# Router logits from the first normalised tile, and a regrouped TensorE sequence

## The chip, the core and the metric

One core of a Trainium2 chip runs the whole program in one launch. The metric is device time in microseconds, the median of three runs.

## The reference

For 128 batches of 128 tokens with 256 features the reference computes a pre-normalised cross attention with a residual, and then a routed feed-forward block with a residual:

```
x = x + attention(layernorm(x), ctx) @ Wo.T + bo      # 16 heads of 16, softmax
h = layernorm(x)
e = argmax(h @ router_w.T + router_b)                  # one of 32 experts per token
x = x + relu(relu(h @ w1[e] + b1[e]) @ w2[e] + b2[e])
```

## The kernel before

The program has an attention stage and a page stage. The attention stage goes over 32 quads `q` of four batches. Its step `s` attends quad `s`, one batch `u` at a time, and in the same step prepares quad `s+1` (keys, queries, values), normalises `s+2`, and routes earlier quads. Each engine's order is written out by hand in a loop over `s` and `u`, with semaphores between engines (`after` waits until a semaphore has counted up to a quad and an index).

In one batch TensorE (loop at L876) does, in this order: scores for the maxima, second half (`scores_for_max(s, u, 1)`, L791, bf16); the exact scores (L806); the first half of probabilities times values of the batch before (`attend`, L824, into bank `pB`); `max_transpose` (L798), which turns the maxima so that they can be subtracted; the second half of `attend`; `subtract_max` (L815); the first half of the next batch's scores for maxima; three of six matmuls of one projection (`project`, L774); transposes of a normalised tile (L765, into bank `sc0`) in some batches; the values of one batch (L782); and in one batch of four the transpose of the logits (L844) or the ranks (L849 to L853). Then come the output projection (`project_out`, L832) and the other three matmuls of the projection.

VectorE (loop at L689) does per batch: `maxima` of the second half (L595, two reductions), `attended` and `normalise` (transpose L615, reciprocal L619, product `nrm` L621 of two SBUF tiles, transpose L626 to `aT`), `maxima` of the next batch's first half, the low half of the transposed tile (`xnT_lo`, L610: bank minus high half), and `residual` (L604), which adds the projected attention to `xs` and stores `row`. Behind the residual stand, by batch, `stats1` (L586, L589), `slot_sum`, `best` with `choose` (L633 to L645), or `scan` (L649).

ScalarE does the exponentials (L468), the copies out of PSUM (L457, L472, L479, L482), both normalisations (`norm1` L435, `norm2` L444) and the squares for the second one (L452). GpSimd (loop at L393) does `rstd1` and `rstd2` (inverse deviations, L281 to L302), `split` (L316, L318: high and low parts of the context), `add_bo` (L308: output bias added to `xs`), the slot arithmetic (`fresh_pages`, `place`), and `scatter` (L386), which writes the rows to pages of one expert each in DRAM. SyncE issues the loads and fills pages.

The second layer norm is applied in full (`norm2`), its tile is transposed (`xn2T`), and `logits` (L838) multiplies it by the router's weights. Logits of quad `q` are taken in step `q+2`; its rows are scattered in step `q+3`. When all rows are placed, the page table is read (L249) and the page stage runs 160 pages through their experts.

The order of TensorE around the change:

```
project(pq, n, (0, 1) if s < 0 else (0,))      # L942
...
values(s + 1, u)                               # L965
...
project_out(q1, u1)                            # L982
project(pq, n, (1,))                           # L984
```

Of the kernel before, what the change touches and what calls it, by code (L numbers as in the profile page):

```python
# [18 lines left out]
QB = 4  # L19
ROW = 260  # L20
COL_TOKEN, COL_EXPERT, COL_MEAN, COL_RSTD = 256, 257, 258, 259
# [32 lines left out]
def build(nc, x, ctxT, wq, wk, wv, wo, bq, bk, bv, bo, wr, rb, w1, w2, consts, out):  # L54
# [14 lines left out]
    with ctx:  # L69
# [6 lines left out]
        def sem(name):  # L76
# [4 lines left out]
        wo_s = sb("wo_s", [2, D])  # L81
# [3 lines left out]
        bv_s, bo_s, rb_s = sb("bv_s", [D]), sb("bo_s", [D]), sb("rb_s", [E])  # L85
        bvT = sb("bvT", [2, P])
        rb4, rbp = sb("rb4", [QB, E]), sb("rbp", [1])
# [3 lines left out]
        xs = sb("xs", [4, QB, D])  # L91
        row = sb("row", [4, QB, ROW])
        xn, xn2 = sb("xn", [QB, D]), sb("xn2", [QB, D])
        xnT = sb("xnT", [2, 2, QB * P], F32R)
        xn2T = sb("xn2T", [2, QB * P])
# [14 lines left out]
        sq2 = sb("sq2", [2])  # L110
# [33 lines left out]
          bvT_done bvT_out bo_done bo_out rbT_done rbp_out rb4_out  # L144
          S_done T_done PV_done O_done V_done proj_done mxT_done xnT_done xn2T_done lg_done lgT_done rk_done
          exp_out V_out proj_out xnT_out xn2T_out lgs_out rk_out xn_out xn2_out
          max_out mxT_out tr_out inv_out nrm_out aT_out x2_out sq_out stat1_out agg1_out xnTl_out
          lg_out top_out eq_out pick_out idx_out hot_out scan_out slot_out
          var1_out pow1_out mr1_out rstd1_out mean2_out sq2_out eps2_out var2_out pow2_out rstd2_out
# [14 lines left out]
        def live(q):  # L164
            return 0 <= q < NQ
# [11 lines left out]
        def xn2T_bank(h):  # L177
            return sc[2 * h]

# [8 lines left out]
        def _(sp):  # L188
            def load_x(q, u):
                sp.dma_start(xs[:, q % 4, u], x[q * QB + u]).then_inc(S[f"ld_x{q % 4}_{u}"], 16)  # L190
# [14 lines left out]
            for dst, src in ((bq_s[:, :], bq), (bk_s[:, :], bk), (bv_s[:, :], bv), (bo_s[:, :], bo), (rb_s[:, :], rb)):  # L205
                sp.dma_start(dst, src).then_inc(S["ld_b"], 16)
            sp.dma_start(wo_s[:, :, :], wo).then_inc(S["ld_wo"], 16)
            for u in range(QB):
                load_x(1, u)
            sp.dma_start(wr_s[:, :, :], wr).then_inc(S["ld_wr"], 16)  # L210
# [11 lines left out]
            load_ctx(3, 0)  # L222
            load_ctx(3, 1)

            for q in range(NQ):
                for u in range(QB):
                    after(sp, "x2_out", 4, q, u)
                    if u == 3 and q >= 2:
                        after(sp, "scattered", 64, q - 2, 63)
# [837 lines left out]
```

## Time and profile before

| | |
|---|---|
| median of three runs (lowest, highest) | 1223.89 us (1223.77, 1226.08) |
| the profiled execution: its time, its span | 1223.15 us, 1221.3 us |
| busy share TensorE, VectorE, ScalarE, GpSimd | 90%, 76%, 70%, 69% |
| chain that ended last | PE 60%, DVE 20%, POOL 7%, DMA 5%, issue 4%, ACT 3% |
| attention stage, its drain, page stage | to about 964, to about 999, to 1221 us |
| granted TensorE clock, mean of the span | 0.972 of full speed |

The chain of waits is followed back from the last instruction; its shares say which engine's work the end hangs on. In the timeline an instruction has its start from the span's beginning and its duration; instructions overlap by their pipelines, so what one costs its engine is the distance to the next start. Matmuls in fp32 take two records each in some groups. A wait stands in brackets, with what ended it.

### The profile page before, as it was taken

The numbers are of one execution on the slowest core, as the hardware profiler recorded it, in microseconds if no ns is written. First come the engines' busy times: TensorE is split into PE (matmuls) and PEld (weight loads), VectorE is DVE, ScalarE is ACT, GpSimd is POOL, SyncE is SP. The second block draws the span as 40 slices with busy tenths as digits, with TensorE's granted clock in tenths as the row PEclk, the third lists the DMA queues.
The fourth block names the chain that finished last, engine by engine and source line by source line (L and its number), as shares of the span: only waits on it lengthen the run. The fifth ranks groups of instructions, "written<-read, shape, count | busy, mean of one in ns | idle before, by whom it ended". The sixth has DMA issues, their size and how long they took to land.

```text
span 1221.3 us, 39225 instructions
## 1 busy us (share of the span) xinstructions
PE 1097.5 (90%) x15399; PEld 845.1 (69%) x15399; DVE 925.0 (76%) x2321; ACT 858.5 (70%) x2020; POOL 847.3 (69%) x1613
## 2 busy tenths in 40 slices
PE   5999999999999999999999999999998419998893
PEld 4777777777777777777777777777776319977772
DVE  4787888888888888888888888888877427866772
ACT  4777777777777777777777777777776306655551
POOL 4544777677777777777777777777764656777776
PEclk9999999999999999999999999999999859999997
DMA  7415222522222222222222222222110136676650
GB/s 243 147 56 121 71 72 71 142 80 76 76 73 79 82 83 75 80 71 72 72 78 74 72 71 72 71 72 72 59 41 29 52 132 205 198 215 205 205 161 17
DMA packets 91156, 120.40 MB, mean 99 GB/s; under 512 B 14096, under 2 KB 73883, under 8 KB 90781
## 3 DMA queue, kind: packets, MB, share of 16 engines
q1 hardware_dynamic: 77150, 84.04, 24.2%
q0 software_dynamic: 13824, 33.85, 7.7%
q8 instruction: 124, 2.03, 0.7%
q14 instruction: 58, 0.48, 0.1%
HBM read 60.61 MB, written 59.31 MB: 98 GB/s over the span
## 4 chain that ended last, share of the span: by engine, by line
PE 60%; DVE 20%; POOL 7%; DMA 5%; issue 4%; ACT 3%; SPq 1%; POOLq 0%; DVEq 0%; ACTq 0%
PE pB L832 10%; PE pA L774 9%; PE pB L824 8%; PE sc L782 7%; DVE mx L595 6%; PE sc L806 5%; POOL out L419 4%; PE sc L765 4%; PE sc L815 3%; ACT arena L468 3%; DVE nrm L621 3%; PE m L791 3%; PE sc L1000 3%; DMA out<-arena 2%; PE m L798 2%
## 5 line engine op out<-in xcount | busy, mean ns | idle before, releaser
L595 DVE TENSOR_REDUCE mx<-m 128x4 bf16<-128x512 f32 x512 | 322.6, 670 | 10.7 <-PE m L791 10.5
L468 ACT ACTIVATE arena<-sc 128x512 f32<-128x512 f32 x512 | 264.5, 603 | 47.5 <-PE sc L815 47.5
L419 POOL DMA_INDIRECT out<-arena x160 | 157.0, 981 | 60.9 <-issue 31.1
L615 DVE STREAM_TRANSPOSE tr<-pB 128x512 f32<-128x512 f32 x128 | 91.8, 717 | 106.3 <-PE pB L824 106.3
L806 PE MATMUL sc<-qk 32*128 32x256 f32 x2048 | 167.0, 397 | 0.5 <-DVE rbp L674 0.5
L824 PE MATMUL pB<-arena 128*32 128x128 f32 x4096 | 159.8, 276 | 1.5 <-issue 1.0
L386 POOL DMA_INDIRECT pages<-row,slot_i x128 | 130.4, 1019 | 40.0 <-issue 37.0
L832 PE MATMUL pB<-wo_s,aT 128*128 128x256 f32 x512 | 138.0, 392 | 8.7 <-DVE aT L626 8.7
L824 PEld LDWEIGHTS pB<-arena 128*32 128x32 f32 x4096 | 99.0, 109 | 44.6 <-issue 43.6
L774 PE MATMUL pA<-cHi,wqkv 128*128 128x512 f32 x252 | 119.0, 474 | 9.4 <-DVE wqkv L660 9.4
L774 PE MATMUL pA<-xnT,wqkv 128*128 128x512 f32 x372 | 124.7, 443 | 0.0
L554 ACT ACTIVATE arena<-sc 128x256 f32<-128x256 f32 x160 | 61.5, 384 | 84.8 <-PE sc L991 81.8
L504 ACT ACTIVATE mxT<-m 128x128 bf16<-128x128 f32 x128 | 35.6, 278 | 115.9 <-PE m L798 115.9
L806 PEld LDWEIGHTS sc<-qk 32*128 32x128 f32 x2048 | 115.4, 186 | 0.7 <-ACT arena L472 0.7
L782 PE MATMUL sc<-wqkv,cHi 128*128 128x256 f32 x512 | 108.3, 303 | 2.5 <-ACT arena L468 0.9
L832 PEld LDWEIGHTS pB<-wo_s,aT 128*128 128x128 f32 x512 | 89.2, 194 | 21.3 <-DVE aT L626 14.6
L791 PE MATMUL m<-qk 32*128 32x128 bf16 x2048 | 101.8, 216 | 1.9 <-ACT qk L482 1.8
L1000 PE MATMUL sc<-arena,xs 128*128 128x128 f32 x640 | 99.1, 278 | 0.0
L791 PEld LDWEIGHTS m<-qk 32*128 32x128 bf16 x2048 | 63.5, 93 | 48.8 <-issue 46.3
L352 POOL TENSOR_TENSOR step_d<-run,ends 128x32 f32<-128x32 f32 x32 | 8.1, 254 | 128.1 <-DVE run L649 128.1
L734 DVE TENSOR_SCALAR arena<-arena 128x256 f32<-128x256 f32 x160 | 71.0, 444 | 32.0 <-DMA arena<-pages 31.7
L991 PE MATMUL sc<-cst,arena 128*128 128x128 f32 x320 | 62.8, 279 | 30.5 <-DVE arena L734 30.2
(141 smaller groups left out, 2714.9 us busy)
## 6 DMA issues: line engine op xcount, KB each, us to landing
arena<-pages SPq DMA_DIRECT2D x160, 130.0 KB
cT<-ctxT SPq DMA_DIRECT2D x64, 256.0 KB, 3.8
xs<-x_in SPq DMA_DIRECT2D x128, 128.0 KB, 3.3
pages<-empty SPq DMA_DIRECT2D x120, 130.0 KB, 3.1
pages<-empty SPq DMA_DIRECT2D x1, 5200.0 KB, 19.8
out<-arena POOLq DMA_INDIRECT x160
w2s<-w SPq DMA_DIRECT2D x1, 2080.0 KB
qk<-w SPq DMA_DIRECT2D x1, 2064.0 KB, 8.2
```

The costliest lines, as they stand in the source:

```text
L386: pool.indirect_dma_start(pages, bass.IndirectOffsetOnAxis(slot_i[:, u:u + 1], 0), row[:, q % 4, u, :], None, bounds_check=last_slot, oob_ ...
L419: pool.indirect_dma_start(out_rows, bass.IndirectOffsetOnAxis(pr[:, r, COL_TOKEN:COL_TOKEN + 1].bitcast(U32), 0), pr[:, r, 0:D], None, bou ...
L468: act.activation(pt[:, u % 2, g].rearrange("p i k -> p (i k)"), sc[g][:, :], ACT.Exp).then_inc(S["exp_out"], 1)
L595: ins = dve.tensor_reduce(mx[:, 32 * g:32 * g + 4], mb[i][:, :].rearrange("p (h k) -> p h k", h=4), AX.X, ALU.max)
L615: dve.transpose(tr[:, :], pB[:, :]).then_inc(S["tr_out"], 1)
L774: ins = pe.matmul(proj_bank(q, n)[:, :], wqkv[:, w, a, i, c * P:(c + 1) * P], src[:, i, :], start=(i == 0 and (a, b) == HI_LO[0]), stop=(i ...
L782: ins = pe.matmul(sc[1][:, 0:D], (cHi, cLo)[a][:, q % 2, i, u * P:(u + 1) * P], wqkv[:, 2, b, i, :], start=(i == 0 and (a, b) == HI_LO[0]) ...
L791: ins = pe.matmul(mb[i][:, j * P:(j + 1) * P], qMh[rows, q % 2, m, c, u * P:(u + 1) * P], kTh[rows, q % 2, c, u * P:(u + 1) * P], start=Tr ...
L806: pe.matmul(dst, kT[rows, q % 2, c, u * P:(u + 1) * P], qM[rows, q % 2, :, c, u * P:(u + 1) * P], start=(c == 0), stop=False, skip_group_c ...
L824: ins = pe.matmul(pB[32 * g:32 * g + 32, j * P:(j + 1) * P], vs[:, q % 2, u, h, :], pt[:, u % 2, g, j, :], start=True, stop=True)
L832: ins = pe.matmul(pB[:, 0:D], aT[:, i, :], wo_s[:, i, :], start=(i == 0), stop=(i == 1))
L1000: ins = pe.matmul(sc[2 + n % 2][:, 0:P], w1p[:, n % W1R, i * HID:i * HID + P], pnT[:, n % DEEP, i * P:(i + 1) * P], start=(i == 0), stop=( ...
```

## The change

The router's logits are no longer computed from the second normalised tile. With the router's weights centred over the features, the mean of the second layer norm drops out of the product, and its inverse deviation can be multiplied in afterwards:

- Setup: `centre_router` subtracts from `wr_s` its mean over features and then over experts. `wo_s` gets 32 more columns, the product of the output weights and the centred router weights; `bo_s` gets 32 more, the bias times the router weights. These products, with their transposes and copies, stand in step -1 on TensorE and VectorE.
- Quad `q`'s first normalised tile, transposed in fp32 (`xnTf`), is multiplied by the router's weights in step `q-1`, batch 1, transposed, multiplied by the deviation (`sd1`, new in `rstd1`), and stored beside `x` in `xs` (`x_logits`, VectorE).
- `project_out` has 288 columns instead of 256, and `residual` adds 288: the last 32 are logits without the scale. `best` multiplies them by `rstd` and adds the router's bias: two more VectorE instructions. `add_bo` adds 288 columns.
- `norm2`, its eight transposes per quad, `xn2T_copy` and `logits_across` go. `squares` writes to a tile of its own.
- `xnT_copy` is two instructions: bank to `xnTf`, `xnTf` to `xnT`; `xnT_lo` subtracts from `xnTf` in SBUF, no longer from the bank.
- All six matmuls of a projection stand together ahead of the values, and the output projection is last in a batch.
- Routing comes one quad earlier: logits' use, ranks and `place` in step `q+1`, scatter in step `q+2`. `rstd2` works on four batches at once. `slot_sum`, `choose`, `scan` and the statistics of batches 0 and 1 move to the place behind the second maxima.
- Rows have their four columns of metadata in front of `x`, not behind it.

```
 def rstd1(q):
     ...
+    pool.tensor_tensor(sd1[:, q % 2, :], v, r, ALU.mult).then_inc(S["std1_out"], 1)
...
 for s in range(-1, NQ + 2):                                    # GpSimd, after
+    if live(s - 2):
+        slots_as_integers(s - 2)
+        scatter(s - 2)
+    if live(s - 1):
+        rstd2(s - 1)
     if s >= 0 and live(s + 2):
         split(s + 2)
     if live(s + 1):
         add_bo(s + 1)
+    if live(s - 1):
+        meta(s - 1)
+    if live(s + 3):
+        rstd1(s + 3)
+    if live(s - 1):
+        fresh_pages(s - 1)
+        place(s - 1)
...
 def xnT_copy(q, h):                                            # ScalarE
-    act.activation(xnT[:, 0, :, 2 * P * h:2 * P * (h + 1)], xnT_bank(q, h)[:, :].rearrange("p (c t) -> p c t", c=2),
-                   ACT.Copy).then_inc(S["xnT_out"], 1)
+    act.activation(xnTf[:, :, at], xnT_bank(q, h)[:, :].rearrange("p (c t) -> p c t", c=2), ACT.Copy).then_inc(S["xnTf_out"], 1)
+    after(act, "xnTf_out", 2, q, h)
+    act.activation(xnT[:, 0, :, at], xnTf[:, :, at], ACT.Copy).then_inc(S["xnT_out"], 1)
...
+def x_logits(q):                                               # VectorE
+    after(dve, "lgT_done", 1, q, 0)
+    after(dve, "std1_out", 1, q, 0)
+    if q >= 4:
+        after(dve, "x2_out", 4, q - 4, 3)
+    dve.tensor_tensor(xs[:, q % 4, :, D:D + E], sc[3][:, 0:P].rearrange("p (u e) -> p u e", e=E),
+                      sd1[:, q % 2, :].unsqueeze(2).to_broadcast([P, QB, E]), ALU.mult).then_inc(S["lg_out"], 1)
...
 def best(q):
-    after(dve, "lg_out", 1, q, 0)
+    after(dve, "rstd2_out", 1, q, 0)
+    if q >= 1:
+        after(dve, "eq_out", 1, q - 1, 0)
+    own("scaled_out", q + 1, dve.tensor_tensor(lg[:, :, :], row[:, q % 4, :, X0 + D:X0 + D + E],
+                                               row[:, q % 4, :, COL_RSTD].unsqueeze(2).to_broadcast([P, QB, E]), ALU.mult))
+    own("z_out", q + 1, dve.tensor_tensor(lg[:, :, :], lg[:, :, :], rb_s[:, :].unsqueeze(1).to_broadcast([P, QB, E]), ALU.add))
...
         maxima(s, u, 1)                                        # VectorE's loop
+        if u == 0 and live(s - 2):
+            slot_sum(s - 2)
+        if u == 2 and live(s - 1):
+            choose(s - 1)
+        if u == 3 and live(s - 1):
+            scan(s - 1)
+        if u < 2 and live(s + 3):
+            stats1(s + 3, (u,))
...
 def project_out(q, u):                                         # TensorE
-        ins = pe.matmul(pB[:, 0:D], aT[:, i, :], wo_s[:, i, :], start=(i == 0), stop=(i == 1))
+        ins = pe.matmul(pB[:, 0:D + E], aT[:, i, :], wo_s[:, i, :], start=(i == 0), stop=(i == 1))
...
-        project(pq, n, (0, 1) if s < 0 else (0,))
+        project(pq, n)
...
-    if live(pq) and s >= 0:
-        project(pq, n, (1,))
```

VectorE between batch 1's residual and batch 2's attention, before (names are tiles; `m` and `pB` are PSUM banks, `row` the stored rows, `lg` logits, `mx` maxima):

```order
L604 SCALAR_TENSOR_TENSOR row<-pB,xs 128x256 [waits scattered,xb_out,O_done]
L633 TENSOR_REDUCE top<-lg 128x4 [waits lg_out]
L634 TENSOR_TENSOR eq<-lg,top 128x128 [waits top_out]
L639 TENSOR_TENSOR eq<-eq,cst 128x128 [waits eq_out]
L642 TENSOR_REDUCE idx<-eq 128x4 [waits expert_out,pick_out]
L645 TENSOR_TENSOR hot<-cst,idx 128x128 [waits own_slots,idx_out]
L595 TENSOR_REDUCE mx<-m 128x4 [waits S_done]
L595 TENSOR_REDUCE mx<-m 128x4
L615 STREAM_TRANSPOSE tr<-pB 128x512 [waits PV_done]
```

and now:

```order
L570 SCALAR_TENSOR_TENSOR row<-pB,xs 128x288 [waits scattered,xb_out,O_done]
L609 TENSOR_TENSOR lg<-row 128x128 [waits eq_out,rstd2_out]
L611 TENSOR_TENSOR lg<-lg,rb_s 128x128 [waits scaled_out]
L612 TENSOR_REDUCE top<-lg 128x4 [waits z_out]
L613 TENSOR_TENSOR eq<-lg,top 128x128 [waits top_out]
L561 TENSOR_REDUCE mx<-m 128x4 [waits S_done]
L561 TENSOR_REDUCE mx<-m 128x4
L618 TENSOR_TENSOR eq<-eq,cst 128x128 [waits eq_out]
L621 TENSOR_REDUCE idx<-eq 128x4 [waits expert_out,pick_out]
L624 TENSOR_TENSOR hot<-cst,idx 128x128 [waits own_slots,idx_out]
L581 STREAM_TRANSPOSE tr<-pB 128x512 [waits PV_done]
```

Four instructions, two of them new, stand between residual and maxima, and the last three of the choice stand behind the maxima.

VectorE between batch 2's residual and batch 3's attention, now (before, `scan` stood at the end of batch 3, behind its residual and the statistics of one batch):

```order
L570 SCALAR_TENSOR_TENSOR row<-pB,xs 128x288 [waits O_done]
L552 BN_STATS st<-xs 128x6 [waits ld_x3_2,agg1_out]
L552 BN_STATS st<-xs 128x6 [waits ld_x3_3]
L555 BN_AGGR ag<-st 128x2 [waits stat1_out] x2
L561 TENSOR_REDUCE mx<-m 128x4 [waits S_done]
L561 TENSOR_REDUCE mx<-m 128x4
L628 SCALAR_TENSOR_TENSOR run<-fresh,run,zer 128x32 [waits fresh_out]
L581 STREAM_TRANSPOSE tr<-pB 128x512 [waits PV_done]
```

The `scan` now stands ahead of the attention's transpose and waits for GpSimd's `fresh`.

GpSimd from the end of `place` to the scatter, before:

```order
L281 TENSOR_SCALAR rs<-ag 128x4 [waits xn_out,agg1_out]
L283 TENSOR_TENSOR rs<-rs,half 128x4 [waits var1_out]
L285 TENSOR_TENSOR nm<-ag,rs 128x4 [waits pow1_out]
L287 TENSOR_SCALAR nm<-nm 128x4 [waits mr1_out]
L316 CAST cHi<-cT 128x1024 [waits V_done,ld_c1,ld_c0]
L318 TENSOR_TENSOR cLo<-cT,cHi 128x1024 [waits ctx_hi]
L376 CAST slot_i<-slot 128x4 [waits slot_out,scattered]
L308 TENSOR_TENSOR xs<-xs,bo_s 128x1024 [waits xn_out]
```

and now, from the end of `rstd2` to `rstd1`, with `fresh_pages` next:

```order
L296 TENSOR_TENSOR row<-row 128x4 [waits pow2_out]
L311 CAST cHi<-cT 128x1024 [waits V_done,ld_c1,ld_c0]
L313 TENSOR_TENSOR cLo<-cT,cHi 128x1024 [waits ctx_hi]
L303 TENSOR_TENSOR xs<-xs,bo_s 128x1152 [waits lg_out,xn_out]
L320 TENSOR_SCALAR expert<-idx 128x4 [waits idx_out]
L322 CAST row<-tok 128x4 [waits tok_out]
L324 CAST row<-expert 128x4 [waits expert_out]
L325 TENSOR_SCALAR tok<-tok 128x4
L274 TENSOR_SCALAR vr<-ag 128x4 [waits lg_out,xn_out,agg1_out]
L276 TENSOR_TENSOR rs<-vr,half 128x4 [waits var1_out]
```

`split` and `add_bo` follow directly on `rstd2`, and `rstd1` stands between them and `fresh_pages`.

## Rows read from the trace of the kernel before

**Rows 1.** Timeline, GpSimd and VectorE: start us, us, engine line op out<-in, count.

```profile
531.80 2.39 POOL L308 TENSOR_TENSOR xs<-xs,bo_s 128x1024 f32<-128x1024 f32 x1
...
533.26 1.21 DVE L621 TENSOR_TENSOR nrm<-tr,inv 128x256 f32<-128x256 f32 x1
...
855.53 1.22 DVE L621 TENSOR_TENSOR nrm<-tr,inv 128x256 f32<-128x256 f32 x1
```

**Rows 2.** Timeline of TensorE over two batches, [idle before it <-releaser].

```profile
524.23 0.24 PE L798 MATMUL m<-ident_b,mx 128*32 128x128 bf16 x4
...
526.64 0.60 PE L765 MATMUL sc<-cst,xn 128*128 128x128 f32 x4
...
527.82 0.33 PE L844 MATMUL sc<-cst,lgs 128*128 128x128 f32 x1
...
527.98 1.03 PE L832 MATMUL pB<-wo_s,aT 128*128 128x256 f32 x4
...
531.47 0.24 PE L798 MATMUL m<-ident_b,mx 128*32 128x128 bf16 x4
...
532.65 0.96 PE L774 MATMUL pA<-xnT,wqkv 128*128 128x512 f32 x3
...
533.45 0.60 PE L765 MATMUL sc<-cst,xn 128*128 128x128 f32 x4
...
533.80 0.48 PE L782 MATMUL sc<-wqkv,cHi 128*128 128x256 f32 x2
...
539.36 0.24 PE L798 MATMUL m<-ident_b,mx 128*32 128x128 bf16 x4 [0.69 <-DVE mx L595]
```

**Rows 3.** Timeline of VectorE in the same quad.

```profile
528.29 0.69 DVE L610 TENSOR_TENSOR xnT<-sc,xnT 128x512 fp32r<-128x512 f32 x1 [0.19 <-ACT xnT L457]
...
529.05 0.42 DVE L604 SCALAR_TENSOR_TENSOR row<-pB,xs 128x256 f32<-128x256 f32 x1
...
536.53 0.28 DVE L633 TENSOR_REDUCE top<-lg 128x4 f32<-128x128 f32 x1
...
538.02 1.28 DVE L595 TENSOR_REDUCE mx<-m 128x4 bf16<-128x512 f32 x2
...
540.11 0.72 DVE L615 STREAM_TRANSPOSE tr<-pB 128x512 f32<-128x512 f32 x1 [0.81 <-PE pB L824]
...
541.98 1.25 DVE L595 TENSOR_REDUCE mx<-m 128x4 bf16<-128x512 f32 x2
...
543.95 0.42 DVE L604 SCALAR_TENSOR_TENSOR row<-pB,xs 128x256 f32<-128x256 f32 x1 [0.72 <-PE pB L832]
...
545.18 1.26 DVE L595 TENSOR_REDUCE mx<-m 128x4 bf16<-128x512 f32 x2
```

**Rows 4.** Timeline of TensorE at the start: six projection matmuls in one stretch.

```profile
18.71 1.56 PE L774 MATMUL m<-xnT,wqkv 128*128 128x512 f32 x6
```

**Rows 5.** Timeline of GpSimd, and one row of ScalarE, in the same quad.

```profile
526.09 0.45 POOL L281 TENSOR_SCALAR rs<-ag 128x4 f32<-128x4 f32 x1
...
528.22 1.04 POOL L316 CAST cHi<-cT 128x1024 fp32r<-128x1024 f32 x1
...
529.84 0.22 ACT L452 ACTIVATION_READ_ACCUMULATOR xn<-row 128x1 f32 x1
...
543.38 0.25 POOL L337 TENSOR_TENSOR need<-rks,room 128x32 f32<-128x32 f32 x1 [1.00 <-ACT rks L500]
...
544.15 0.30 POOL L341 TENSOR_SCALAR fresh<-fresh 128x32 f32<-128x32 f32 x1
```

**Rows 6.** Timeline of TensorE, and a 2 us stretch of the drain (busy time, PEclk, DMA).

```profile
936.41 0.33 PE L844 MATMUL sc<-cst,lgs 128*128 128x128 f32 x1 [1.93 <-ACT arena L468]
...
938.00:940.00 2.00, 2.00 (x25) 1.33 (x23) 1.47 (x5) 0.54 (x3) 0.73 (x2) 0.50 0.00 0
```

**Rows 7.** Timeline of the drain: last output projection, read of the page table.

```profile
963.63 1.13 PE L832 MATMUL pB<-wo_s,aT 128*128 128x256 f32 x4 [0.81 <-DVE aT L626]
...
999.46 0.58 SPq L249 DMA_DIRECT2D arena<-pages  x1
```

More of the change, by code:

```diff
@@ L392, in _ @@
             split(1)
-            for s in range(-1, NQ + 3):
-                if live(s - 1):
-                    rstd2(s - 1, 0)
-                if live(s - 3):
-                    place(s - 3)
-                if live(s + 2):
-                    rstd1(s + 2)
+            rstd1(1)
+            for s in range(-1, NQ + 2):
+                if live(s - 2):
+                    slots_as_integers(s - 2)
+                    scatter(s - 2)
+                if live(s - 1):
+                    rstd2(s - 1)
                 if s >= 0 and live(s + 2):
                     split(s + 2)
-                if live(s - 3):
-                    slots_as_integers(s - 3)
                 if live(s + 1):
                     add_bo(s + 1)
-                if live(s - 3):
-                    if live(s - 1):
-                        after(pool, "sq_out", 4, s - 1, 3)
-                    scatter(s - 3)
                 if live(s - 1):
-                    rstd2(s - 1, 1)
-                if live(s - 2):
-                    meta(s - 2)
-                    fresh_pages(s - 2)
+                    meta(s - 1)
[4 more added lines that the diff above has]
+                    place(s - 1)
             for n in range(PAGES):
@@ L538, in _ @@
                             norm1(s + 2, v)
-                    if u in (0, 2) and live(s - 1):
-                        norm2(s - 1, u)
-                        norm2(s - 1, u + 1)
                     if live(q1):
@@ L688, in _ @@
             query_masks()
-            for s in range(-2, NQ + 3):
+            for s in range(-2, NQ + 2):
                 for u in range(QB):
@@ new lines, in output_bias, with router_weights @@
+                ins.then_inc(S["setup_products"], 1)
+                for c in range(2):
+                    for i in range(2):
+                        ins = pe.transpose(sc[2][:, (2 * c + i) * P:(2 * c + i + 1) * P], wo_s[:, i, c * P:(c + 1) * P], ident)
+                ins.then_inc(S["setup_products"], 1)
+            def router_weights():
+                pe.wait_ge(S["wr_centred"], 4)
+                pe.wait_ge(S["setup_copies"], 2)
+                for c in range(2):
+                    for i in range(2):
+                        ins = pe.matmul(sc[0][:, c * E:(c + 1) * E], won_s[:, i, c * P:(c + 1) * P], wr_s[:, i, :],
+                                        start=(i == 0), stop=(i == 1))
+                ins.then_inc(S["setup_products"], 1)
+                pe.wait_ge(S["bo_out"], 1)
+                for c in range(2):
+                    ins = pe.transpose(pB[:, c * P:(c + 1) * P], bo_s[:, c * P:(c + 1) * P], ident)
+                ins.then_inc(S["setup_products"], 1)
+                logits(0)
+                after(pe, "lgs_out", 1, 0, 0)
+                logits_transpose(0)
@@ L872, in _, with router_bias @@
+            def router_bias():
+                pe.wait_ge(S["setup_copies"], 4)
+                for i in range(2):
+                    ins = pe.matmul(pB[:, D:D + E], boT[:, i, :], wr_s[:, i, :], start=(i == 0), stop=(i == 1))
+                ins.then_inc(S["setup_products"], 1)
             pe.wait_ge(S["ld_cst"], 16)
@@ L930, in _ @@
                     if live(pq):
-                        if u == 0 and live(s - 2):
-                            after(pe, "lgs_out", 1, s - 2, 0)
+                        if u == 1 and s >= 0 and live(s + 1):
+                            after(pe, "lgs_out", 1, s + 1, 0)
                         elif s >= 0:
```

306 lines of the change are left out of this document (136 added, 170 removed).

## The prediction

> **What bounds the kernel now.** Read the busy shares and the chain of waits first: TensorE is the busiest engine and carries most of the chain, so only what lengthens or shortens its sequence, or makes it wait, counts. The stage repeats every four batches (a quad): the same VectorE instruction stands at 533.26 and, 11 quads on, at 855.53 [rows 1], so a quad takes 29.30 us. Then read one quad instruction by instruction. My mark is M(u), the moment when TensorE transposes the maxima of batch u (L798), since everything later in the batch hangs on it: M(0) at 524.23, M(1) at 531.47, M(2) at 539.36 [rows 2]. M(2) stands behind a wait of 0.69 for VectorE, which ran five small routing instructions in front of the maxima (536.53 to 538.02) [rows 3]. So VectorE is the second bound, met once in a quad. GpSimd has time to spare, but holds VectorE once in a quad, 26 times in all: `nrm`, 0.42 us long elsewhere, takes 1.21, and ends 0.28 after GpSimd's `xs` addition (531.80 + 2.39 = 534.19, against 534.47) [rows 1]. The runs' median is 1223.89; the profiled execution took 1223.15, and sums are made against that.
>
> **TensorE's own work.** From M to the row transposes are 1.98 us with three projection matmuls (531.47 to 533.45) and 2.41 with logits (524.23 to 526.64), so logits cost 0.43; four transposes 0.35 (533.45 to 533.80); the transpose of logits 0.16 (527.82 to 527.98); and of the 3.75 from M(0) to the output projection, 0.83 are left for the values [rows 2]. Six projection matmuls in one stretch take some 1.50 (1.56, the last one's tail partly hidden [rows 4]), against 0.80 for three (532.65 to 533.45): 0.70 more before the output projection, and not after it. The change takes out eight of the transposes in a quad (0.70) and adds 32 columns to the output projection: an eighth of about 0.68, 0.08 a batch. It puts logits into batch 1. From M to the output projection I get 1.98 + 0.70 + 0.83 = 3.51, and so: u0 and u3, with transposes, 3.86; u1, with logits and their transpose, 4.10; u2, with the ranks (an estimate of 0.20, by the 0.16 of the one transpose), 3.71.
>
> **VectorE behind it.** Before, the second half of a projection stood behind the output projection and covered the residual. That cover is gone. The residual starts 1.07 after the output projection's start (527.98 to 529.05), 1.15 with the wider one, and lasts 0.42; the second maxima and their transpose follow in 1.34 (538.02 to M at 539.36) [rows 2, 3]. This is 2.91 from an output projection to the next M, in every batch. Between residual and maxima stand, after u1, the four instructions of `best` (of five in 1.49, so 1.2), and after u2 two statistics (543.95 to 545.18 less the residual: 0.81) [rows 3]. `choose`, `slot_sum`, `scan` and the other statistics move into the idle 0.75 after the maxima (539.36 to 540.11) [rows 2, 3] and cost nothing while that holds. From M to M:
> u0 3.86 + 2.91 = 6.77; u1 4.10 + 2.91 + 1.20 = 8.21; u2 3.71 + 2.91 + 0.81 = 7.43; u3 6.77. Sum 29.18 against 29.30: taken alone, the change is worth 0.1 a quad. The removed work on ScalarE (norm2 and its copies) gains nothing, as ScalarE already waits for TensorE. Its longer path now (squares behind the residual, then the projection's copy) ends near or before the next M, so I cost it at nothing, at most 0.3 a quad.
>
> **The scan waits for GpSimd (u3).** `scan` stands between maxima and the attention's transpose and needs `fresh`, which GpSimd makes behind `rstd1`, and that needs the statistics that end when the maxima of u3 start, 1.3 before M(3). `rstd1` takes 2.13 (526.09 to 528.22) and its new product 0.2; `fresh` 1.07 (543.38 to 544.15 and 0.30) [rows 5]. So `fresh` is there 2.1 after M(3), scan takes 0.25, and the transpose starts at 2.35 rather than 0.75. It and the first maxima take 3.12 (540.11 to 541.98, and 1.25), the remainder of `xnT` 0.69, residual 0.42, maxima 1.34 [rows 3]: M(0) of the next quad comes 7.92 after M(3). **+1.15 a quad.**
>
> **`best` meets the addition of the bias (u1).** Counted from M(0): the residual of the last batch starts at 3.86 + 1.15 = 5.0, its squares are summed 1.0 later (529.05 to 529.84 + 0.22) [rows 3, 5], and then `rstd2` runs for four batches at once: six small instructions with one power, by the four of `rstd1` about 2.6, to 8.6. `split` takes 3.45 (528.22 to 531.80, less a cast), to 12.0; the addition to `xs` 2.39 x 1152/1024 = 2.69, to 14.7 [rows 1, 5]. VectorE: M(1) 6.77, output projection 10.87, residual 12.0, so `best` begins at 12.45 with a product of two SBUF tiles, as `nrm` is. The addition is 0.4 under way. If the product waits as `nrm` did, it ends at 14.98 and not 12.74: **+2.24 a quad**. The three behind it and the maxima wait in turn, and TensorE with them. The Trainium skill says this as a rule (SBUF — State Buffer, "Who interferes with whom"): VectorE with two SBUF inputs and GpSimd reading SBUF lock each other out for a whole instruction. By that rule the remainder of `xnT`, which now reads SBUF twice, would also wait for one of `place`'s short instructions in u3, 0.2 to 0.4 a quad more; the trace shows only the long GpSimd instructions doing it.
>
> **The clock.** From the output projection to the next M TensorE itself needs 3.49 less the second half of the projection (527.98 to 531.47, less 0.70) [rows 2], so 2.8; M(2) now comes 2.91 + 1.20 + 2.24 = 6.35 after it. TensorE is idle for 3.5 us before M(2). Nothing like it stands in the main stage, where the granted clock is 1.00. In the drain an idle 1.93 us (before 936.41) is followed by a stretch at 0.50 (938 to 940) [rows 6], that is 1.2 GHz. Those 2 us cost 1.0 where TensorE sets the pace, and it does between M(2) and M(3). Bounds are 0 and 2.0; I take **+1.4 a quad**. The Trainium skill (TensorE: Matmul & The Clock Gate, "Why this matters for your kernels") warns of idle gaps between bursts of matmuls, after which the clock falls back. By that rule every quad has such a fall, as in my sum; the trace agrees in one place, outside the main stage.
>
> **Start and drain.** The start gains setup products, transposes and copies in a ring between TensorE, VectorE and ScalarE: 0 to 8, taken as 4 (twelve small matmuls at the price of the transposes, 1.1, and a few hand-overs). In the drain 35.8 us pass from the last output projection to the read of the page table (963.63 to 999.46) [rows 7]. Routing now runs one quad earlier and without norm2, eight transposes and late logits: statistics 2, rest of a scatter 1.5, `rstd2` 2.6, `best` and `choose` 2.1, ranks 1.2, `fresh_pages` and `place` 5.2, last scatter and landing 8: some 22.5. **-13**, bounds -6 and -18. The page stage is untouched. SyncE's context loads move in its queue and now wait for `split` of the same step (12.0); the next `split` starts some 30 later, so they stay covered.
>
> **Sum.** Quads 1 to 28 have both waits: 28 x (-0.12 + 1.15 + 2.24 + 1.40) = 28 x 4.67 = 131. Quad 29 has the addition but not `rstd1`: about 3. 1223.15 + 131 + 3 + 4 - 13 = **1348 us**.
>
> **Rivals.**
> - Faster, the other side: neither wait bites. `best` passes freely if the addition is over by 12.45 or begins after 13.7, so if GpSimd is 2.3 earlier or 1.7 later than I count; and the scan costs nothing if VectorE's slack takes it. Then 1223.15 - 28 x 0.12 + 4 - 13 = 1211; were VectorE never late, TensorE alone (3.9 + 2.8 a batch, near 26.8 a quad, in 28 quads) would give 1144. For: GpSimd idles enough, and my count has ten steps. Against: both gaps are larger than any step's error, and the lock came in nearly every quad. 0.20.
> - Only the scan waits: 1223.15 + 28 x 1.03 - 9 = 1243. For: `best`'s operands differ in shape from `nrm`'s. 0.13.
> - Both waits, clock stays at 1.00: 1223.15 + 28 x 3.27 + 2 - 9 = 1308. For: the one case at hand is from the drain, where TensorE had little else to do. 0.20.
> - Both, and the low clock lasts through u3 too (2.5 to 3 a quad): 1385. 0.07.
> - The gains and losses cancel within 0.2% of 1223.9 (what a measurement of this kernel can tell from no change): 0.02.
>
> **How the numbers follow.** The forecast gets 0.38, and by itself lies between 1325 and 1375. Slower is 0.38 + 0.13 + 0.20 + 0.07 = 0.78, faster 0.20, same 0.02. The range leaves out the faster half of the faster cases and most beyond 1385: 1205 to 1385.
>
> **What would show it.** Right: a period near 34 us; the first product of `best` lasting 2.3 to 2.6 and ending just after GpSimd's addition; scan idle some 2 us behind `fresh`; each maxima transpose in u2 behind a wait above 3 us; the granted clock under 1.00 in the main stage; the page table read about 22 after the last output projection. Wrong: a period under 29.3, `best` at 0.3 an instruction, or TensorE without waits at M.

## The result, and the profile of the changed kernel

| | before | changed |
|---|---|---|
| median, timed side by side (lowest, highest) | 1224.93 us (1223.77, 1226.08) | 1362.42 us (1357.60, 1362.93) |
| ratio, with its 95% interval | | 1.111 (1.109 to 1.114) |
| the profiled execution: time, span | 1223.15, 1221.3 us | 1362.93, 1361.1 us |
| M(0) to M(0), quads 2 to 27, mean | 29.35 us | 34.05 us |
| granted TensorE clock, mean of the span | 0.972 | 0.936 |

The change makes the kernel 11% slower; 1348 was forecast, 1205 to 1385 the range. The page of the changed kernel has TensorE's busy share down by 7 points, and VectorE with nearly a third of the chain of waits (20% before). These are its busy shares, its row of granted clock in 40 slices, and its chain by engine and by line:

```profile
PE 1125.3 (83%) x15164; PEld 861.5 (63%) x15164; DVE 1028.3 (76%) x2424; ACT 808.2 (59%) x1860; POOL 823.5 (61%) x1453
...
PEclk9999999999999998999999999999999876999997
...
PE 42%; DVE 30%; POOL 10%; issue 8%; DMA 6%; ACT 4%; SPq 1%; POOLq 0%; DVEq 0%
PE pA L764 14%; DVE mx L561 9%; PE pB L821 5%; DVE lg L609 5%; PE sc L771 4%; PE pB L813 4%; POOL out L410 3%; DVE xnT L576 3%; DMA out<-arena 3%; PE sc L804 3%; DMA arena<-pages 2%; POOL rs L276 2%; DVE row L570 2%; PE sc L1005 2%; PE m L787 2%
```

One instruction stands out in that chain: `lg` at L609, the first product of `best`, holds 5% of the span. The marks M of one quad, from the timeline of TensorE, in the order u2, u3, u0, u1, u2 (the last number in a row is the idle time before it; they answer to [rows 2]):

```profile
563.73 0.24 PE L787 MATMUL m<-ident_b,mx 128*32 128x128 bf16 x4 [3.35 <-DVE mx L561]
...
572.76 0.24 PE L787 MATMUL m<-ident_b,mx 128*32 128x128 bf16 x4 [0.79 <-DVE mx L561]
...
580.63 0.24 PE L787 MATMUL m<-ident_b,mx 128*32 128x128 bf16 x4 [0.41 <-DVE mx L561]
...
587.56 0.24 PE L787 MATMUL m<-ident_b,mx 128*32 128x128 bf16 x4
...
597.79 0.24 PE L787 MATMUL m<-ident_b,mx 128*32 128x128 bf16 x4 [3.33 <-DVE mx L561]
```

| from M to M, us | forecast | this quad |
|---|---|---|
| u0 | 6.77 | 6.93 |
| u1, with the held product | 10.45 | 10.23 |
| u2, with the low clock | 7.43 + 1.40 = 8.83 | 9.03 |
| u3, with the scan's wait | 7.92 | 7.87 |
| quad | 33.97 | 34.06 |

The held product of u1, in the timelines of GpSimd (first three rows) and VectorE (the others). Below, this holding is called the lock. The addition that holds the product ends at 592.79 + 2.62 = 595.41, the product at 593.05 + 2.51 = 595.56:

```profile
589.28 1.04 POOL L311 CAST cHi<-cT 128x1024 fp32r<-128x1024 f32 x1
590.40 2.43 POOL L313 TENSOR_TENSOR cLo<-cT,cHi 128x1024 fp32r<-128x1024 f32 x1
592.79 2.62 POOL L303 TENSOR_TENSOR xs<-xs,bo_s 128x1152 f32<-128x1152 f32 x1
...
589.36 1.25 DVE L587 TENSOR_TENSOR nrm<-tr,inv 128x256 f32<-128x256 f32 x1
...
592.67 0.46 DVE L570 SCALAR_TENSOR_TENSOR row<-pB,xs 128x288 f32<-128x288 f32 x1 [0.22 <-PE pB L821]
...
593.05 2.51 DVE L609 TENSOR_TENSOR lg<-row 128x128 f32<-128x128 f32 x1
595.60 0.29 DVE L611 TENSOR_TENSOR lg<-lg,rb_s 128x128 f32<-128x128 f32 x1
```

The addition of the router's bias next to it (L611), of the same size and with GpSimd's addition out of the way, takes 0.29. `nrm` at 589.36 is held too (1.25 against 0.42), by the cast that ends at 590.32.

In quads 2, 9 and 19 GpSimd's addition begins 0.3 to 0.4 later. There the same product passes, and the instruction behind it is held. Quad 9, GpSimd and then VectorE:

```profile
353.86 2.69 POOL L303 TENSOR_TENSOR xs<-xs,bo_s 128x1152 f32<-128x1152 f32 x1
...
353.69 0.38 DVE L609 TENSOR_TENSOR lg<-row 128x128 f32<-128x128 f32 x1
354.10 2.60 DVE L611 TENSOR_TENSOR lg<-lg,rb_s 128x128 f32<-128x128 f32 x1
```

So in this trace it is the one that starts second that waits, and M(1) to M(2) is as long (10.31 to 10.40).

The wait of u3, timeline of VectorE: the second maxima, and `scan`, which stands idle for 2.08 and starts 2.02 after M(3) at 572.76.

```profile
571.45 1.26 DVE L561 TENSOR_REDUCE mx<-m 128x4 bf16<-128x512 f32 x2
574.78 0.47 DVE L628 TENSOR_TENSOR_SCAN run<-fresh,run,zer 128x32 f32<-128x32 f32 x1 [2.08 <-POOL fresh L336]
```

The clock, as stretches (from:to, length, busy TensorE, granted clock, DMA). The first holds M(2) at 563.73 and is low in its second half only; the third is the time from 1.2 us after M(2) at 597.79 on:

```profile
561.45:568.28 6.83, 4.55 (x54) 0.75 0.06 20
568.28:598.99 30.71, 25.63 (x426) 1.00 0.23 71
598.99:602.41 3.42, 3.42 (x12) 0.51 0.02 5
```

A stretch at 1.2 GHz stands near M(2) in 25 of the 26 quads from 2 to 27: in 24 of them it lasts 3.4 us and begins 0.0 to 1.8 us after M(2), in quad 14 it lasts 6.8 and begins before M(2), and quad 26 has none. Six projection matmuls in it take 2.93 (at 564.91), in u1 1.66. The drain, the rows that answer to [rows 7]:

```profile
1116.95 1.45 PE L821 MATMUL pB<-wo_s,aT 128*128 128x288 f32 x4 [2.08 <-DVE aT L592]
...
1138.13 0.57 SPq L241 DMA_DIRECT2D arena<-pages  x1
```

Where the 139.7 us between the two spans lie (before, then changed): to the first M 30.30, 37.45: **+7.2**; quads 0 and 1 53.03, 65.21: **+12.2**; quads 2 to 27 763.2, 885.3: **+122.1**; from there to the last output projection 117.1, 129.0: **+11.9**; to the read of the page table 35.8, 21.2: **-14.6**; the page stage 221.9, 223.0: **+1.1**.

### The profile page after: what moved, and what is told of

Its sections match the earlier page's. It is cut to its first block, busy times and chain, and to the rows that moved or that the text cites. A ratio compares the mean times of both kernels' runs of the same rounds, so it can differ in the third digit from the quotient of the medians.

```text
span 1361.1 us, 38518 instructions
## 1 busy us (share of the span) xinstructions
PE 1125.3 (83%) x15164; PEld 861.5 (63%) x15164; DVE 1028.3 (76%) x2424; ACT 808.2 (59%) x1860; POOL 823.5 (61%) x1453
## 4 chain that ended last, share of the span: by engine, by line
PE 42%; DVE 30%; POOL 10%; issue 8%; DMA 6%; ACT 4%; SPq 1%; POOLq 0%; DVEq 0%
PE pA L764 14%; DVE mx L561 9%; PE pB L821 5%; DVE lg L609 5%; PE sc L771 4%; PE pB L813 4%; POOL out L410 3%; DVE xnT L576 3%; DMA out<-arena 3%; PE sc L804 3%; DMA arena<-pages 2%; POOL rs L276 2%; DVE row L570 2%; PE sc L1005 2%; PE m L787 2%
## 5 line engine op out<-in xcount | busy, mean ns | idle before, releaser
L821 PE MATMUL pB<-wo_s,aT 128*128 128x288 f32 x512 | 153.0, 422 | 17.9 <-DVE aT L592 17.9
L813 PE MATMUL pB<-arena 128*32 128x128 f32 x4096 | 163.5, 280 | 0.6 <-DVE row L570 0.6
L787 PE MATMUL m<-ident_b,mx 128*32 128x128 bf16 x512 | 30.8, 231 | 142.4 <-DVE mx L561 137.9
L764 PE MATMUL pA<-xnT,wqkv 128*128 128x512 f32 x372 | 133.2, 507 | 0.0
L570 DVE SCALAR_TENSOR_TENSOR row<-pB,xs 128x288 f32<-128x288 f32 x128 | 58.0, 453 | 91.6 <-PE pB L821 91.6
L787 PEld LDWEIGHTS m<-ident_b,mx 128*32 128x32 bf16 x512 | 13.1, 93 | 176.3 <-DVE mx L561 176.3
L274 POOL TENSOR_SCALAR vr<-ag 128x4 f32<-128x4 f32 x32 | 7.5, 234 | 189.8 <-DVE ag L555 189.5
L433 ACT ACTIVATE junk<-row 128x256 f32<-128x256 f32 x128 | 53.3, 416 | 108.9 <-DVE row L570 108.9
L771 PE MATMUL sc<-wqkv,cHi 128*128 128x256 f32 x512 | 114.4, 317 | 0.9 <-ACT arena L448 0.9
L764 PE MATMUL pA<-cHi,wqkv 128*128 128x512 f32 x252 | 97.7, 428 | 9.5 <-DVE wqkv L639 9.5
```

What stands on the lines that cost most here:

```text
L570: dve.scalar_tensor_tensor(row[:, q % 4, u, X0:X0 + D + E], pB[:, 0:D + E], 1.0, xs[:, q % 4, u, :], ALU.mult, ALU.add, accum_out=row[:, q ...
L764: ins = pe.matmul(proj_bank(q, n)[:, :], wqkv[:, w, a, i, c * P:(c + 1) * P], src[:, i, :], start=(i == 0 and (a, b) == HI_LO[0]), stop=(i ...
L771: ins = pe.matmul(sc[1][:, 0:D], (cHi, cLo)[a][:, q % 2, i, u * P:(u + 1) * P], wqkv[:, 2, b, i, :], start=(i == 0 and (a, b) == HI_LO[0]) ...
L813: ins = pe.matmul(pB[32 * g:32 * g + 32, j * P:(j + 1) * P], vs[:, q % 2, u, h, :], pt[:, u % 2, g, j, :], start=True, stop=True)
L821: ins = pe.matmul(pB[:, 0:D + E], aT[:, i, :], wo_s[:, i, :], start=(i == 0), stop=(i == 1))
```

## The experiments

Times are medians beside runs of the kernel before on the same chip (1223.75, 1223.51 or 1222.59 us in the three sets of runs). Theory: the held product, the scan's wait and the low clock make the change slow. Rivals are in the expectations.

**1. The addition out of the way of `best`.**

```diff
-                if live(s + 1):
-                    add_bo(s + 1)
                 if live(s - 1):
                     meta(s - 1)
+                if live(s + 1):
+                    if s >= 0:
+                        after(pool, "nrm_out", 4, s, 1)
+                    add_bo(s + 1)
```

> GpSimd's addition of the output bias goes behind meta and waits for the second nrm of batch 1, so that it cannot be under way when best begins. Theory (GpSimd's long addition holds best's first product, and the long idle time of TensorE behind it brings the half clock): the product lasts about 0.3 us instead of 2.5, M(1) to M(2) falls from 10.2 to about 8.1 us, the idle time before M(2) from 3.3 to about 1.2 us, the granted clock stays at 1.00 in the main stage, and the time falls by 28 x (2.2 + 1.0 to 1.6), to 1255 to 1275 us. Rival (the product is slow by its own form, or because four columns are spread over 16): the product still lasts 2.5 us and the time stays within 10 us of 1362. Second rival (the addition then meets another instruction with two SBUF inputs, nrm of batch 2): half of the gain at most, 1310 or more.

Measured: 1245.66 us (1244.47 to 1250.51), ratio 1.019 (1.016 to 1.022): 117 us back for one instruction that runs 5 us later. The groups of the product, of the changed kernel first, then of this run:

```profile
L609 DVE TENSOR_TENSOR lg<-row 128x128 f32<-128x128 f32 x32 | 69.5, 2171 | 3.1 <-POOL row L296 3.1
```

```profile
L611 DVE TENSOR_TENSOR lg<-row 128x128 f32<-128x128 f32 x32 | 9.3, 292 | 3.6 <-POOL row L296 3.6
```

u1 falls from 10.25 to 8.00, u2 from 9.03 to 7.50 (medians), and no low clock is left in quads 2 to 27. So 2.25 us a quad were the lock and 1.53 the clock behind it. The time is below the 1255 to 1275 expected because quads 0, 1 and those after 27 had such losses too: of the 117.6 us between the two profiled spans 96.7 lie in quads 2 to 27, 6.6 ahead of quad 2 and 14.3 behind quad 27.

**2. TensorE's idle time filled.** Nine matmuls that no one reads, between the output projection and M(2):

```diff
+                    if u == 2 and s >= 1 and live(s + 1):
+                        after(pe, "proj_out", 4, bq_, bn)
+                        for _ in range(9):
+                            pe.matmul(pA[:, :], ident_b[:, :], sel_b[:, :, :].rearrange("p a t -> p (a t)"), start=True, stop=True)
                     if live(s):
                         max_transpose(s, u)
```

> In batch 2 nine bf16 matmuls of 128 x 512, whose result nothing reads, stand between the output projection and the transpose of the maxima, where TensorE otherwise idles 3.3 us. Nothing else is changed. Theory (TensorE's own idle time there brings the stretch at half clock that stands in every quad): the granted clock stays at 1.00 in the main stage, M(2) to M(3) falls from 9.0 to about 7.5 us, and the time falls by 28 x 1.4, to 1318 to 1325 us. Rival (the low clock comes from something else, or costs nothing because VectorE sets the pace then): 1355 to 1370 us. If the filler is longer than the idle time the gain is smaller by 28 times the excess.

Measured: 1312.27 us (1307.42 to 1314.48), 50 us less, with more work on the busiest engine. Around the filler, and the granted clock of 33 us of this run:

```profile
565.02 2.12 PE L931 MATMUL pA<-sel_b,ident_b 128*128 128x512 bf16 x9 [0.61 <-ACT qk L462]
...
567.77 0.24 PE L787 MATMUL m<-ident_b,mx 128*32 128x128 bf16 x4 [0.64 <-DVE mx L561]
...
540.00:573.00 33.00, 30.02 (x457) 1.00 0.23 66
```

u1 stays at 10.25, as it must, since the lock is still there; u2 falls to 7.49. So it is TensorE's own idle time that brings the low clock. Its size is 1.54 a quad: quads 2 to 27 are 38.8 us shorter together, and the rest of the gain lies at both ends of the stage.

**3. `fresh` first.** The scan's wait alone taken away.

```diff
+                if live(s - 1):
+                    fresh_pages(s - 1)
                 if live(s + 3):
                     rstd1(s + 3)
                 if live(s - 1):
-                    fresh_pages(s - 1)
                     place(s - 1)
```

> GpSimd makes fresh ahead of rstd1, and place stays behind it. Theory (the scan waits for fresh because rstd1 waits for the statistics): scan has no wait, M(3) to M(0) falls from 7.9 to about 6.8 us, and the time falls by 28 x 1.1, to about 1331 us (1325 to 1345). Rival (scan's wait only covers work of TensorE or ScalarE that would set the pace a little later): under 10 us. The lock in batch 1 and the low clock stay as they are.

Measured: 1363.22 us (1353.68 to 1367.04): nothing, where I expected 31 us. The wait did go: u3 fell from 7.86 to 6.93. But u2 rose from 9.03 to 10.03. TensorE at M(2) in this run, and the granted clock just around it and over the whole low stretch:

```profile
561.92 0.30 PE L788 MATMUL m<-ident_b,mx 128*32 128x128 bf16 x4 [3.36 <-DVE mx L562]
...
561.50:563.00 1.50, 1.08 (x20) 0.50 0.00 0
...
561.70:568.50 6.80, 6.58 (x66) 0.56 0.00 0
```

The idle time is the same 3.36, but the low stretch now begins before M(2) and lasts 6.8 us instead of 3.4, in each of 26 quads. This miss asked for a run of its own:

**4. `fresh` first, with the filler.** Both edits above.

> The changed kernel with both the idle time of TensorE filled in batch 2 (as in the run with the nine matmuls) and fresh made ahead of rstd1. Theory (taking the scan's wait away gained nothing by itself only because the low clock then lasted twice as long): with the clock at 1.00 it gains its 0.93 us a quad, so 26 us less than the filler alone, 1286 us (1280 to 1292), and M(3) to M(0) is 6.93. Rival (without the scan's wait something else is late in the next batches): within 8 us of 1312.

Measured: 1282.71 us (1281.37 to 1285.09). That is 29.6 less than the filler alone; u3 is 6.93, u2 7.50, and the granted clock stays at 1.00 in quads 2 to 27. So the scan's wait was on the path all along, and the clock took back what its removal gave.

**5. Both edits of GpSimd's order** (1 and 3), without the filler.

> The two edits of GpSimd's order together: the addition behind meta and behind the second nrm of batch 1, and fresh ahead of rstd1. Theory (these two waits and the clock are all that makes the change slow): a quad of 29.2 to 29.5 us, no low clock in the main stage, and 1211 to 1225 us, that is the time of the kernel before or some 10 us less. Rival (part of the 4.7 us a quad lies in work that I counted as free): 1235 to 1260 us, with VectorE late before some M that had no wait for it before.

Measured: 1219.70 us (1217.31 to 1221.01), ratio 0.996 (0.994 to 0.998). A quad takes 29.47: u0 6.93, u1 8.00, u2 7.50, u3 7.04. The two places in GpSimd's program account for the whole of the 11%. What is left of the change is 0.4% faster than the kernel before, and not by its period (29.47 against 29.35): its drain takes 22.0 us where the kernel before takes 35.8, and it loses most of that again at the start and in the quads.

**6. `best` without scaling and bias.** Its first instruction with two SBUF inputs is now the comparison; the logits are neither scaled by rstd nor given the router's bias.

```diff
-                own("scaled_out", q + 1, dve.tensor_tensor(lg[:, :, :], row[:, q % 4, :, X0 + D:X0 + D + E],
...
-                own("top_out", q + 1, dve.tensor_reduce(top[:, :], lg[:, :, :], AX.X, ALU.max))
-                dve.tensor_tensor(eq[:, :, :], lg[:, :, :], over_e(top), ALU.is_equal).then_inc(S["eq_out"], 1)
+                own("top_out", q + 1, dve.tensor_reduce(top[:, :], row[:, q % 4, :, X0 + D:X0 + D + E], AX.X, ALU.max))
+                dve.tensor_tensor(eq[:, :, :], row[:, q % 4, :, X0 + D:X0 + D + E], over_e(top), ALU.is_equal).then_inc(S["eq_out"], 1)
```

> The changed kernel without the scaling of the logits by rstd and without the router's bias, so without the first two of best's four instructions in batch 1; the routing differs. VectorE's first instruction after the residual has one input there, the second (the comparison) two. Theory (GpSimd's addition holds any instruction of VectorE with two SBUF inputs until it ends): the maximum over the logits takes 0.3, the comparison then lasts some 2 us and ends with the addition; M(2) comes only about 0.6 to 0.9 earlier, the low clock stays or is shorter, and the time falls by 15 to 45 us from 1362. Rival (only the product is slow, by its spread-out operand): the comparison lasts 0.3, M(1) to M(2) falls to 7.4, the clock stays at 1.00 and the time falls by more than 100 us.

Measured: 1311.40 us (1304.04 to 1318.24), 51 us less than the changed kernel. Its groups of the maximum (one input) and of the comparison (two):

```profile
L610 DVE TENSOR_TENSOR eq<-row,top 128x128 f32<-128x128 f32 x32 | 67.8, 2120 | 1.1
...
L609 DVE TENSOR_REDUCE top<-row 128x4 f32<-128x128 f32 x32 | 9.0, 281 | 3.6 <-POOL row L296 3.6
```

The comparison, 0.29 elsewhere, takes the product's place; the maximum starts under the same addition and passes in 0.28. So it is not the form of the product, and what is held is the instruction with two inputs from SBUF. The gain is above my 45 for a reason worth seeing. These are M(2) and M(3) of two quads of this run:

```profile
536.87 0.24 PE L784 MATMUL m<-ident_b,mx 128*32 128x128 bf16 x4 [2.39 <-DVE mx L561]
544.37 0.24 PE L784 MATMUL m<-ident_b,mx 128*32 128x128 bf16 x4 [0.78 <-DVE mx L561]
...
568.45 0.24 PE L784 MATMUL m<-ident_b,mx 128*32 128x128 bf16 x4 [2.39 <-DVE mx L561]
577.44 0.24 PE L784 MATMUL m<-ident_b,mx 128*32 128x128 bf16 x4 [0.78 <-DVE mx L561]
```

The idle time is 2.39 in both, but M(2) to M(3) takes 7.50 in one quad and 8.99 in the next: with 2.4 us idle the low clock came in 14 of the 26 quads, in two of them for 6.8 us (M(2) to M(3) 10.27).

**7. The regrouped projection alone**, in the kernel before.

```diff
-                        project(pq, n, (0, 1) if s < 0 else (0,))
+                        project(pq, n)
...
-                    if live(pq) and s >= 0:
-                        project(pq, n, (1,))
```

> The kernel before with one part of the change alone: each projection's six matmuls in one stretch ahead of the output projection. Theory (this part costs the cover of the residual): each batch is longer by up to 0.7, less what VectorE's wait for its input to the output projection hides: 30.5 to 31.4 a quad against 29.35, so 1255 to 1289 us. Rival (the order of the projection alone is worth nothing): 1220 to 1230 us.

Measured: 1272.25 us (1269.38 to 1273.25), ratio 1.040 (1.038 to 1.041). A quad takes 30.99; from M to M it is 7.85, 8.07, 7.36 and 7.72 against 7.31, 7.85, 7.17 and 7.03. TensorE now waits 1.39 before M(2), where [rows 2] have 0.69, and 0.60 to 0.75 before the other three marks, where it hardly waited. The second half of the projection did cover the residual.

**8. The projection cut in two again**, on the version of run 5.

```diff
-                        project(pq, n)
+                        project(pq, n, (0, 1) if s < 0 else (0,))
...
                     if live(q1):
                         project_out(q1, u1)
+                    if live(pq) and s >= 0:
+                        project(pq, n, (1,))
```

> The changed kernel with GpSimd's order mended as in the third run, and each projection cut in two again: three matmuls ahead of the output projection, three behind it, as the kernel before has them; logits, values and the position of the output projection's inputs stay as changed. Theory (by the prediction's own work: the 0.70 of a second half belongs behind the output projection, where VectorE's residual and maxima keep TensorE waiting anyway): from M to M 6.7 in batches 0, 2 and 3, where TensorE alone is then the bound, and 7.5 in batch 1; 27.7 a quad against 29.5, so about 1219.7 - 28 x 1.8 = 1170 us (1160 to 1185). Rival (the regrouping is neutral, because the output projection cannot start before its transposed input comes from VectorE anyway): within 8 us of 1220. A second rival: ScalarE gets the projection later, its copy comes too late for the maxima of the next batch, and the time is above 1220.

Measured: 1199.79 us (1199.30 to 1201.19), ratio 0.981 (0.979 to 0.982): faster than both kernels, but by 20 us and not the 50 I expected. A quad takes 28.78: 6.68, 7.99, 7.27, 6.78. u0 and u3 came to TensorE's own work, as said; u1 and u2 hardly moved. In them the output projection starts only 0.17 and 0.23 earlier after M, not 0.70, because something else stands ahead of it that waits for ScalarE. In u1 it is the transpose of logits (first row ScalarE's four exponentials, which end at 532.82, then TensorE; M(1) is at 529.27):

```profile
530.75 2.07 ACT L451 ACTIVATE arena<-sc 128x512 f32<-128x512 f32 x4
...
532.59 0.28 PE L775 MATMUL sc<-wqkv,cLo 128*128 128x256 f32 x1
532.87 0.33 PE L836 MATMUL sc<-cst,lgs 128*128 128x128 f32 x1
533.03 1.14 PE L825 MATMUL pB<-wo_s,aT 128*128 128x288 f32 x4
```

In u2 the ranks stand behind the exponentials in the same way. In u1 `best` also lost what was won, since its product now begins while GpSimd's `split` is still at work (mean 463 ns against 293 in run 5). And behind the output projection u1 takes 4.23 and u2 3.83 to the next M, where u0 takes 3.55: VectorE ends these two. The next run takes that away.

**9. VectorE's small work spread**, on the version of run 8.

```diff
                     if u == 2 and live(s - 1):
+                        best_of(s - 1)
                         choose(s - 1)
                     if u == 3 and live(s - 1):
                         scan(s - 1)
-                    if u < 2 and live(s + 3):
+                    if u != 2 and live(s + 3):
                         stats1(s + 3, (u,))
...
                     if u == 2 and live(s + 3):
-                        stats1(s + 3, (2, 3))
+                        stats1(s + 3, (2,))
```

(`best_of` is the last two instructions of `best`; GpSimd makes `rstd1` after `place`.)

> The split version with VectorE's small work spread: of best only scaling and bias stay ahead of the second maxima of batch 1, its other two instructions go behind them, in front of choose; of the two statistics of batch 2 one goes behind scan in batch 3; and GpSimd makes rstd1 behind place, since the last statistics now come later. Nothing is left out. Theory (where VectorE is late, each of its instructions between residual and maxima costs its time, and the same instruction behind the maxima is free until the output projection's input is late): M(1) to M(2) falls from 8.0 to 7.4 us, M(2) to M(3) from 7.3 to 6.9 us, and the time from 1199.8 to about 1172 us (1168 to 1178). Rival (the attention's transpose, now 0.6 us later in batch 2 and 0.4 in batch 3, delays the output projection by as much): under 8 us of gain.

Measured: 1177.23 us (1172.33 to 1182.33), ratio 0.964 (0.961 to 0.967). A quad takes 27.96: 6.68, 7.46, 7.09, 6.68. The chain of waits, first of run 8, then of this one:

```profile
PE 63%; DVE 14%; ACT 8%; issue 6%; POOL 4%; DMA 4%; SPq 1%; POOLq 0%; DVEq 0%
```

```profile
PE 73%; ACT 7%; DMA 6%; POOL 5%; DVE 4%; issue 4%; SPq 1%; POOLq 0%; DVEq 0%
```

From the output projection to the next M u1 takes 3.70 and u2 3.64, close to the 3.55 of u0, and VectorE has nearly left the path. What is kept of the change here (logits from the first normalised tile, values ahead of the output projection, no second normalisation) together with the spread work is 45 us, 3.6%, faster than the kernel before. How much of that the kernel before would gain by such a spreading alone was not tried: it too has 0.69 of waiting for VectorE before M(2).

## Why the prediction was right, and where it was off

**The lock: right in place, end and size.** I put the end of the product 14.98 us after M(0); it ended at 595.56 - 580.63 = 14.93. I gave it 2.24 a quad; run 1 shows 2.25. The addition was to be 0.4 under way when the product begins, and it is 0.26. That margin is small, but the forecast did not hang on it: in the three quads where the addition comes too late for the product, the next instruction pays. Run 6 shows that the two inputs from SBUF are what counts, as the Trainium skill has it (SBUF — State Buffer, "Who interferes with whom").

**The scan: right, a third too dear.** `fresh` was to be there 2.1 after M(3), and `scan` starts at 2.02. I took 1.15 a quad; between runs 1 and 5 u3 falls by 0.83, because u3 without the wait is 7.04 and not 6.77, and between runs 2 and 4 it falls by 0.94, to 6.93. The 0.11 between the two is the lock again: the remainder of `xnT` in u3 lasts 0.80 in run 5 and 0.69 in run 4.

**The clock: right in place, near in size.** Taken 1.4, measured 1.53 (runs 1 and 2). But I treated it as a fixed price for an idle time. The changed kernel itself, with 3.35 idle, has 7.50 from M(2) to M(3) in quad 26, 9.03 in most, 9.82 in quad 14. Run 3 shows 2.5 a quad for the same idle time, run 6 nothing, 1.5 or 2.8 for one idle time. What decides between them stays open. That the term came near is luck in part: my rival with 2.5 to 3 a quad had a chance of 0.07, and it is what run 3 has after the same idle time.

**TensorE's own work: 29.18 forecast, 29.47 in run 5.** The term that was off is "2.91 from an output projection to the next M, in every batch". In u0 it is 3.10 and in u3 3.21, because the residual starts 1.38 and 1.50 after the output projection and not 1.15. Ahead of it stands the remainder of `xnT`, which now waits for two copies of ScalarE in place of one. I had costed ScalarE's longer path "at nothing, at most 0.3 a quad"; here is where it shows. u0 of the quad above, ScalarE, then VectorE (the output projection starts at 584.47):

```profile
583.95 0.60 ACT L441 ACTIVATE xnTf<-sc 128x512 f32<-128x512 f32 x1 [0.20 <-PE sc L755]
584.58 0.63 ACT L443 ACTIVATE xnT<-xnTf 128x512 fp32r<-128x512 f32 x1
...
585.24 0.69 DVE L576 TENSOR_TENSOR xnT<-xnTf,xnT 128x512 fp32r<-128x512 f32 x1 [0.74 <-ACT xnT L443]
585.85 0.45 DVE L570 SCALAR_TENSOR_TENSOR row<-pB,xs 128x288 f32<-128x288 f32 x1
```

This is read from the timeline; no run has one copy in place of two. u0 became 6.93 (6.77). u1 was 8.00 (8.21), u2 7.50 (7.43), u3 7.04 (6.77).

**The cover of the residual:** stated as 0.70 a batch before the output projection, and not hidden behind it. Run 7 shows 1.64 a quad and not 2.8: 0.54 and 0.69 in u0 and u3, but only 0.22 and 0.19 in u1 and u2. In those the second half had not been free to begin with: TensorE waited ahead of the output projection anyway, in u2 for ScalarE's exponentials, in u1 for an input that VectorE brought late. In the changed order the sums from M to the output projection do hold (3.86, 4.10 and 3.71 forecast for u0, u1 and u2; 3.83, 3.93 and 3.67 in run 5), since six matmuls outlast ScalarE. Taking 0.70 off each again, as the expectation of run 8 did, was wrong by 30 us.

**The edge of the trace: 7.5 us missing.** The sum had 28 quads at 4.67, from quad 1 on. But the kernel before does not need 29.30 in quads 0 and 1, where routing has not begun; it needs 26.24 and 26.79, and the changed one 31.18 and 34.03. I read the period from the middle of the trace and used it at its edge. Of the 7.5, 3.5 lie in quad 0 and are a lock too, the one of the next paragraph, with 3.4 us of low clock behind it: in runs 1 to 4 and 6, where it does not bite, quad 0 takes 27.7.

**The start: +7.2, where I took 4.** The excess is the same lock, in a place where I did not look for it: the remainder of `xnT`, 0.69 long, reads SBUF twice since the change, and meets GpSimd's subtraction in `split` (first row GpSimd, second VectorE):

```profile
17.18 2.34 POOL L313 TENSOR_TENSOR cLo<-cT,cHi 128x1024 fp32r<-128x1024 f32 x1
...
17.42 2.65 DVE L576 TENSOR_TENSOR xnT<-xnTf,xnT 128x512 fp32r<-128x512 f32 x1 [0.37 <-ACT xnT L443]
```

TensorE then stands idle for 2.75 before 20.17, and from 29.0 to 35.8 its clock is 0.50. No run was made to try this link, but the others show it by chance. In runs 2, 4, 5, 8 and 9 the remainder starts 0.16 to 0.22 ahead of the subtraction and passes in 0.66 to 0.69; the subtraction then takes 2.7 to 2.8 and not 2.34, and the first M comes at 33.3 to 35.0. In runs 1, 3 and 6 it starts 0.05 to 0.25 behind, takes 2.6 to 2.8, and the first M comes at 38.0 to 38.8, here at 37.45. The kernel before has it at 30.30. So the setup alone costs 3.0 to 4.7, as forecast, and which of the two instructions comes first decides over some 4 us. I had costed this instruction in u3 only, at 0.2 to 0.4 behind `place`; there it is 0.81 against 0.69, so 0.1.

**The drain: 22.5 forecast, 21.2 measured**, with 35.8 before; the last quads and the page stage were 4 and 1 us longer than in the sum. Together, 125 us were forecast over the profiled execution of before and 139.7 measured: 7.5 from quads 0 and 1, 3.2 from the start, 4.2 and 1.1 at the end, 0.7 in the middle, less 1.6 in the drain. In the middle the errors cancel: the batches were 0.29 longer than forecast (29.47 against 29.18) and the clock 0.13 dearer, but the scan 0.32 cheaper.

## What to carry to other kernels

When a change gives a small VectorE instruction two inputs in SBUF, or moves a long GpSimd instruction, lay the two timelines side by side: if it starts second, it costs what is left of the other one, whatever its own size, and everything queued behind it on VectorE and TensorE is late by as much. A few tenths of a microsecond decide which of the two is first. A wait that makes the busiest engine idle for some microseconds can cost a second time through its clock, so a repair may show its worth only together with another (run 3 alone: nothing; on top of the filler: 30 us). And an instruction between the residual and the next maxima is on the path here, while the same one just behind the maxima is free as long as TensorE's own work does not set the pace (run 9: 0.6 us of work moved, u1 0.53 shorter): look for such a place before looking for less work.

## What the runs showed of the hardware that I had not expected

- A GpSimd cast, with one input, holds VectorE as well: `nrm` at 589.36 takes 1.25, the cast 589.28 to 590.32; in run 1 `nrm` at 560.15 takes 1.25 beside the cast of 560.08 to 561.12. The issue of an indirect DMA by GpSimd does not: `nrm` at 582.42 takes 0.42, in the middle of the one of 581.86 to 582.99.
- The low clock after an idle time of TensorE is no fixed price. Idle 3.35 before M(2): mostly 3.4 us at half clock, once 6.8 and once none (the changed kernel), or 6.8 us in every quad (run 3). Idle 2.39: a low stretch in 14 of 26 quads (run 6). Idle 1.39 to 1.45 in run 7, and 1.1 in runs 1 and 5: none in quads 2 to 27.
- The kernel before pays for a lock too. In quad 7 `nrm` of u1 takes 0.43 and not 1.21, and the quad 28.79 and not 29.30.
- Useless matmuls in the idle time paid for themselves: 50 us for nine of them a quad (run 2).
